# Re-ordering the opening of a four-layer modulated convolution kernel

## The chip, the cores and the metric
One core of one Trainium2 chip. The metric is the device time of one execution in microseconds, here the median of three runs.

## The reference
```python
def _layer(x, style, w, b, mw, mb, typ):
    s = style @ mw.T + mb
    weight = SCALE * w * s[:, None, :, None]
    demod = lax.rsqrt(jnp.sum(weight * weight, axis=(2, 3)) + EPS)
    weight = weight * demod[:, :, None, None]
    if typ == 'same': out = jax.vmap(_conv_same)(x, weight) + b[None, :, None]
    elif typ == 'upsample': ...  # transposed conv, stride 2, + b, then blur (1, 3, 3, 1)
    elif typ == 'downsample': ...  # blur, then conv of stride 2, + b
    return out
# layers: same, upsample, same, downsample; result is x + layer3(layer2(layer1(layer0(x))))
```
x is 128 samples of 64 channels by 1024 positions in float32, the style 128 samples by 128; each layer has 64 x 64 x 3 weights. The weights differ from sample to sample, since s and demod do.

## The kernel before
All four layers are linear, so the kernel multiplies them into one filter bank per sample, adds the identity, and applies that bank to the sample once; the few positions at the edges are computed layer by layer for 32 samples at a time (`edge`). Float32 is kept by splitting operands into a high float32r part (`high`, `w_high`, `x_high`, casts on ScalarE) and a low remainder (`low`, `w_low`, `x_low`, subtractions on VectorE), with three matmuls for a product (lines 167 to 169) or two where the low part sits in the other half of the partitions (172, 173).

Engine names: PE is TensorE, DVE VectorE, ACT ScalarE, POOL GpSimd, SP the engine that issues most of the DMAs.

Samples go in groups of four. The bank of group g comes out of seven units, `unit(g, 0)` to `unit(g, 6)`: units 0 and 1 turn Q3 (layer 3 scaled by D32) and A2 (layer 2) into Q2, units 2 and 3 with B1 (layer 1 with the blurs summed in, `static_sums`) into G, units 4 to 6 with C (layer 0) into Wf. After each unit VectorE scales the result in PSUM (`full`), ScalarE casts it, VectorE takes the low part, and only then can the unit that reads it start. `w_sum`, `w_high`, `w_low` make the taps W, and SP copies parts of W to the other half of the partitions with nine DMAs per group (`cross`, lines 217 to 227), for which the group's first sample waits. Each sample has 9 matmuls into `ps` (`conv_shared`), a copy into `py`, 15 more (`conv_rest`, one sample behind), and a result on ScalarE. POOL prepares x (`columns`, lines 608 and 609) and the Q3 of later groups (`q3_full`, `q3_low`).

The order is written out by hand, and each engine's queue is in program order: `PROLOGUE` is the list of units ahead of sample 0, `FIRST` those ahead of samples 0 to 3, `SLOTS` those of every later group; four PSUM banks are handed on along this list.

Ahead of the units stands the opening: S = style times mw (line 375), its square, the energies (line 381, three matmuls a layer), the roots and the demodulation factors DD. A factor was made of Sqrt on ScalarE (508, 513, 514), a reciprocal on VectorE (797, 826, 836) and four chained VectorE operations (`newton`, 764 to 767); each link waits for the one in front of it. D32, D10c, D21, inv3 are products of S and DD that `full`, Q3 and the identity need. Layer constants (K1, K2, K3, cv) come from small matmuls (404, 412) and short chains on VectorE (856 to 865) ahead of sample 0.

## Time and profile before
| | |
|---|---|
| median of 3 runs | 686.85 us (686.07 to 687.09) |
| the profiled execution | 686.25 us, span 684.4 us |
| busy over the span | PE 93%, DVE 81%, ACT 62%, POOL 33% |
| mean granted PE clock | 0.982 |
| chain that ended last | PE 71%, DVE 17%, ACT 6%, issue 5%, DMA 1% |
| first matmul of sample 0 / of unit (2, 4) | 55.23 / 76.27 us |

The busy shares are means over stages of different kind: an opening of some 70 us, and 31 groups after it that repeat. A share says nothing of a stage; the tables by stage and the timeline do. Times in the timeline count from the start of the span. The rest of an execution's time, 1.85 us here, lies outside the span.

### The profile page before, as it was taken

What the parts mean: (1) busy time and instruction counts of PE and PEld (TensorE: products, weight loads), DVE (VectorE), ACT (ScalarE), POOL (GpSimd) and SP (SyncE); (2) the same over time, 40 slices, a digit from 0 to 9 for tenths busy, and PEclk for the clock granted to TensorE, in tenths of its full rate; (3) what the DMA queues carried; (4) which work ended last, traced back from release to release, by engine and by line L of the source; (5) the groups of instructions that cost most, each with busy time, mean ns of one, the idle gap of its engine ahead of it and who ended that gap; (6) DMA issues with size and microseconds to landing.
All of it is one profiled execution on the core that took longest, in us unless ns stands there. A gap on an engine that the chain in (4) does not pass through costs nothing.

```text
span 684.4 us, 13324 instructions
## 1 busy us (share of the span) xinstructions
PE 635.5 (93%) x5012; PEld 626.6 (92%) x5012; DVE 551.1 (81%) x836; ACT 425.0 (62%) x713; POOL 225.6 (33%) x246
## 2 busy tenths in 40 slices
PE   5648999999999999989999999989999999989967
PEld 4647999999999999989999999989999999989967
DVE  6897687887978797978979798797988888787961
ACT  3435566576667677476666767556677757655653
POOL 4315232333234333332333333413423333224130
PEclk9987999999999999999999999999999999999999
DMA  6035388667777877757788777757886777768772
GB/s 212 38 89 136 115 231 217 178 192 194 197 197 217 231 205 200 198 167 200 189 231 227 185 194 222 199 169 197 231 215 165 221 207 213 203 166 231 196 206 108
DMA packets 155840, 129.89 MB, mean 190 GB/s; under 512 B 7104, under 2 KB 122176, under 8 KB 155776
## 3 DMA queue, kind: packets, MB, share of 16 engines
q1 hardware_dynamic: 155120, 127.47, 68.6%
q10 hardware_dynamic: 656, 1.57, 0.7%
q8 instruction: 40, 0.66, 0.4%
q14 instruction: 24, 0.20, 0.1%
HBM read 36.47 MB, written 33.82 MB: 103 GB/s over the span
## 4 chain that ended last, share of the span: by engine, by line
PE 71%; DVE 17%; ACT 6%; issue 5%; DMA 1%; POOL 0%; ACTq 0%; DVEq 0%; POOLq 0%
PE py L167 9%; PE py L169 9%; PE py L168 9%; PE ps L167 6%; PE ps L168 6%; PE pg L167 6%; PE ps L169 6%; PE pg L169 6%; PE pg L168 6%; PE pg L172 3%; PE pg L173 3%; DVE W L708 2%; DVE xl L653 1%; ACT xh L437 1%; DVE pg L661 1%
## 5 line engine op out<-in xcount | busy, mean ns | idle before, releaser
L168 PE MATMUL py<-xl,W 128*128 128x256 f32 x640 | 182.5, 285 | 0.0
L167 PE MATMUL py<-xh,W 128*128 128x256 f32 x640 | 182.4, 285 | 0.0
L169 PE MATMUL py<-xh,W 128*128 128x256 f32 x640 | 181.9, 284 | 0.0
L608 POOL TENSOR_TENSOR X<-X 128x514 f32<-128x514 f32 x64 | 73.1, 1142 | 240.3 <-DMA X<-in_xin 238.0
L167 PEld LDWEIGHTS py<-xh,W 128*128 128x128 f32 x640 | 126.9, 198 | 0.0
L168 PEld LDWEIGHTS py<-xl,W 128*128 128x128 f32 x640 | 126.8, 198 | 0.0
L169 PEld LDWEIGHTS py<-xh,W 128*128 128x128 f32 x640 | 126.7, 198 | 0.0
L486 ACT CAST W<-Wf 128x768 fp32r<-128x768 f32 x64 | 53.2, 831 | 111.6 <-PE py L169 103.7
L167 PE MATMUL ps<-xh,W 128*128 128x256 f32 x384 | 114.1, 297 | 8.7 <-issue 5.8
L653 DVE TENSOR_TENSOR xl<-X,xh 128x1548 fp32r<-128x1548 f32 x64 | 114.4, 1787 | 7.4 <-ACT xh L437 6.7
L451 ACT ACTIVATE T<-py,cv,DD 128x512 f32<-128x512 f32 x128 | 99.3, 776 | 22.4 <-PE py L169 22.4
L168 PE MATMUL ps<-xl,W 128*128 128x256 f32 x384 | 110.6, 288 | 0.0
L169 PE MATMUL ps<-xh,W 128*128 128x256 f32 x384 | 110.4, 287 | 0.0
L437 ACT CAST xh<-X 128x1548 fp32r<-128x1548 f32 x64 | 94.8, 1480 | 0.0
L167 PEld LDWEIGHTS ps<-xh,W 128*128 128x128 f32 x384 | 77.0, 200 | 10.8 <-issue 8.8
L708 DVE TENSOR_TENSOR W<-Wf,W 128x768 fp32r<-128x768 f32 x64 | 62.6, 986 | 23.5 <-ACT W L486 23.4
L592 POOL TENSOR_TENSOR Q3l<-Q3f,Q3h 128x256 fp32r<-128x256 f32 x31 | 24.1, 778 | 174.1 <-ACT Q3h L466 174.1
L443 ACT COPY py<-ps 128x512 f32<-128x512 f32 x128 | 76.0, 594 | 5.6 <-PE ps L169 5.6
L169 PEld LDWEIGHTS ps<-xh,W 128*128 128x128 f32 x384 | 77.3, 201 | 0.0
L609 POOL TENSOR_TENSOR X<-X 128x516 f32<-128x516 f32 x64 | 77.2, 1206 | 0.0
L168 PEld LDWEIGHTS ps<-xl,W 128*128 128x128 f32 x384 | 77.0, 201 | 0.0
L475 ACT CAST Q2h<-pg 128x512 fp32r<-128x512 f32 x64 | 27.5, 483 | 65.4 <-DVE pg L661 63.4
(166 smaller groups left out, 1490.5 us busy)
## 6 DMA issues: line engine op xcount, KB each, us to landing
X<-in_xin SPq DMA_DIRECT2D x64, 516.0 KB, 5.2
out<-T SPq DMA_DIRECT2D x64, 512.0 KB, 3.1
W<-W SPq DMA_DIRECT2D x64, 384.0 KB, 4.3
W<-W SPq DMA_DIRECT2D x96, 128.0 KB, 4.4
W<-M SPq DMA_DIRECT2D x96, 128.0 KB, 3.6
W<-W SPq DMA_DIRECT2D x32, 256.0 KB, 4.7
E<-in_ed ACTq DMA_DIRECT2D x1, 768.0 KB, 7.6
XE<-in_xe SPq DMA_DIRECT2D x1, 576.0 KB, 5.0
```

What stands on the lines that cost most here:

```text
L167: eng.matmul(o, wh_, rh, start=first, stop=False, skip_group_check=onto)
L168: eng.matmul(o, wh_, rl, start=False, stop=False, skip_group_check=onto)
L169: return eng.matmul(o, wl_, rh, start=False, stop=last, skip_group_check=onto)
L437: act.copy(xh[:, n % XH], X[:, n % XR, :, 1:4]).then_inc(s_xh, 1)
L443: act.copy(py[b % YR][:, :].rearrange("p (e k) -> p e k", e=2), pm.unsqueeze(1).to_broadcast([128, 2, H])).then_inc(s_ae, 1)
L451: act.activation(T[:, n % TR, q].rearrange("p e k -> p (e k)"), py[b % YR][:, :], ACT.Identity, bias=cv[:, b:b + 1], scale=DD[:, 3, b:b + ...
L475: act.copy(Q2h[:, :, 2 * u:2 * u + k], src).then_inc(s_q2h, 1)
L486: act.copy(taps_of(g, 0, k), Wf[:, :, PARTS[k]]).then_inc(s_wh, 1)
L608: pool.tensor_tensor(x[:, :, 3, 0:XW - 1], x[:, :, 0, 1:XW], x[:, :, 1, 0:XW - 1], ALU.subtract)
L609: pool.tensor_tensor(x[:, :, 2], x[:, :, 0], x[:, :, 1], ALU.subtract).then_inc(s_s, 1)
L653: tt(xl[:, n % XH], X[:, n % XR, :, 1:4], r32(xh[:, n % XH]), ALU.subtract).then_inc(s_xl, 1)
L708: m = tt(taps_of(g, 1, k), Wf[:, :, PARTS[k]], r32(taps_of(g, 0, k)), ALU.subtract)
```

## The change
1. Loads: the tables of S come as `m23` (layers 2 and 3, with the style and the biases in one transfer) and `m01`; `wt` is split (`wt2` alone on ScalarE's queue); `a2`, `wt`, `cw`, `ed` move to SP's queue, `cw`, `eye`, `ed` behind `load(0)`, and `load(2)` behind `xe`.
2. Roots: ScalarE's Abs_reciprocal_sqrt straight from PSUM, then one Newton step of three scalar_tensor_tensor operations; no reciprocal, no Sqrt. S and the energies are done in two parts, energies of layers 0, 1 and 3 in `py`.
3. Order: the prologue has group 0 whole, then (1, 0) and (1, 1). (1, 2) to (1, 6) and all that follow go into `FIRST`, a sample later than before. Constants K2 and K3 on PE stand behind samples 0 and 1 and their chains on VectorE in those samples (`constants`), the edge scales in sample 2 (`edge_scales`). `columns(0)` and `columns(1)` on POOL stand behind B1l and `identity(0)`.

The diff, cut to its core and with the indentation reduced:
```diff
-PROLOGUE = [(0, 0), (0, 1), (0, 2), (0, 3), (1, 0), (1, 1), (0, 4), (0, 5), (0, 6), (1, 2), (1, 3)]
-FIRST = [[(1, 4), (1, 5), (1, 6)], [(2, 0), (2, 1)], [(2, 2)], [(2, 3), (3, 0), (3, 1)]]
+PROLOGUE = [(0, 0), (0, 1), (0, 2), (0, 3), (0, 4), (0, 5), (0, 6), (1, 0), (1, 1)]
+FIRST = [[(1, 2), (1, 3)], [(1, 4), (1, 5), (1, 6)], [(2, 0), (2, 1)], [(2, 2), (2, 3), (3, 0), (3, 1)]]
...
+s_pp, s_ch, s_eps, s_ms, s_sq, s_ss, s_rr, s_sc, s_k0, s_b1, s_bs = (
+    sem(n) for n in ("pp", "ch", "eps", "ms", "sq", "ss", "rr", "sc", "k0", "b1", "bs"))
+PP_S23, PP_S01, PP_E2, PP_E01, PP_E3, PP_K1, PP_K2, PP_K3 = range(1, 9)
+SC_S23, SC_SQ2, SC_S01, SC_D32, SC_K1, SC_D, SC_K2, SC_K3, SC_CV = range(1, 10)
 K_A2, K_C, K_B1, K_B1D = 1, 2, 3, 4
+AT = {2: 0, 0: 1, 1: 2, 3: 3}
...
-for n, dst, src in (("mwt", MW, mwt.rearrange("p (l m) -> p l m", l=4)),
+for n, dst, src in (("m23", MS[:], m23),
                     ("b1", b1w[:, 2 * C:6 * C], b1),
-                    ("bb", BB[:], bb.rearrange("p (k l) -> p k l", k=2)),
+                    ("m01", M01, m01),
                     ("q3", q3s[:], q3.rearrange("p (k o) -> p k o", k=2)),
-                    ("eye", EYE[:], eye)):
+                    ("a2", A2f, a2),
+                    ("wt", WT[:, 1:4], wt.rearrange("p (l t m) -> p l t m", l=3, t=3))):
...
     if n == XR - 1:
-        sp.wait_ge(s_pp, 3)
+        sp.wait_ge(s_pp, PP_E3)
...
-for n in range(XR):
-    load(n)
+load(0)
+for n, dst, src in (("cw", Cf, cw.rearrange("p (d m) -> p d m", d=4)),
+                    ("eye", EYE[:], eye),
+                    ("ed", E[:], ed.rearrange("p (l t m) -> p l t m", l=4, t=3))):
+    sp.dma_start(dst, src).then_inc(s_in[n], 16)
+load(1)
 sp.dma_start(XE[:], xe).then_inc(s_in["xe"], 16)
+load(2)
 for k in range(3):
...
-for n in ("mwt", "st"):
-    pe.wait_ge(s_in[n], 16)
-for l in range(4):
-    m = pe.matmul(ps[:, l * 128:l * 128 + 128], MW[:, l, :], ST, start=True, stop=True)
+pe.wait_ge(s_in["m23"], 16)
+for l in (2, 3):
+    m = pe.matmul(pg[3][:, (l - 2) * 128:(l - 1) * 128], MS[:, (l - 2) * 128:(l - 1) * 128], ST, start=True, stop=True)
 m.then_inc(s_pp, 1)
-def energy(l):
-    o = pe_[:, 0:128] if l == 2 else ps[:, l * 128:l * 128 + 128]
+pe.wait_ge(s_in["m01"], 16)
+for l in (0, 1):
+    m = pe.matmul(ps[:, l * 128:l * 128 + 128], M01[:, l * 128:l * 128 + 128], ST, start=True, stop=True)
+m.then_inc(s_pp, 1)
+def energy(o, l):
     for t in range(3):
-        m = pe.matmul(o, SQ[:, l, t], tmp[0:64, l, :], start=t == 0, stop=t == 2)
+        m = pe.matmul(o, SQ[:, AT[l], t], tmp[0:64, l, :], start=t == 0, stop=t == 2)
     return m
...
 pe.wait_ge(s_sc, SC_SQ2)
-energy(2).then_inc(s_pp, 1)
+energy(pe_[:, 0:128], 2).then_inc(s_pp, 1)
 pe.wait_ge(s_sq, 2)
-pe.wait_ge(s_ss, 1)
-for l in (0, 1, 3):
-    m = energy(l)
-m.then_inc(s_pp, 1)
+pe.wait_ge(s_ss, 2)
+energy(py[0][:, 0:128], 0)
+energy(py[0][:, 128:256], 1).then_inc(s_pp, 1)
+energy(py[1][:, 0:128], 3).then_inc(s_pp, 1)
 pe.wait_ge(s_a2, 1)
-for i in range(YR):
-    pe.matmul(py[i][:, :], A2h[:, 0:128], A2h[:, :], start=True, stop=True)
 for x in PROLOGUE[:2]:
...
 pe.wait_ge(s_b1, 1)
-for x in PROLOGUE[2:6]:
+for x in PROLOGUE[2:4]:
     unit(*x)
+pe.wait_ge(s_cl, 1)
+for x in PROLOGUE[4:]:
+    unit(*x)
+pe.wait_ge(s_sc, SC_D)
+for i in range(YR):
+    pe.matmul(py[i][:, :], A2h[:, 0:128], A2h[:, :], start=True, stop=True)
 pe.wait_ge(s_in["ed"], 16)
-pe.wait_ge(s_sc, SC_K1)
 for t in range(3):
...
 m.then_inc(s_pp, 1)
-pe.wait_ge(s_cl, 1)
-for x in PROLOGUE[6:]:
-    unit(*x)
-for l, k, at in ((2, 1, SC_K2), (3, 3, SC_K3)):
+def constant(l, k, at):
     pe.wait_ge(s_sc, at)
     for t in range(3):
-        m = pe.matmul(pe_[0:64, 0:128], WT[:, l, t], tmp[0:64, k, :], start=t == 0, stop=t == 2)
+        m = pe.matmul(pe_[0:64, 0:128], WT[:, AT[l], t], tmp[0:64, k, :], start=t == 0, stop=t == 2)
     m.then_inc(s_pp, 1)
...
+    if b == 0:
+        constant(2, 1, SC_K2)
+    elif b == 1:
+        constant(3, 3, SC_K3)
     if i == 3 and g % 2 == 0:
...
 def _(act):
-for n, dst, src in (("st", ST, st), ("wt", WT, wt.rearrange("p (l t m) -> p l t m", l=4, t=3)),
...
-act.wait_ge(s_one, 1)
-act.activation(one[:], one[:], ACT.Sqrt)
-act.wait_ge(s_in["wt"], 16)
-twice = lambda l: WT[:, l].unsqueeze(2).to_broadcast([64, 3, 2, C])
...
-act.activation(pairs(2), twice(2), ACT.Square).then_inc(s_sq, 1)
+def square(a, e):
+    return act.activation(SQ[:, a:e].rearrange("p l t (d m) -> p (l t) d m", d=2),
+                          WT[:, a:e].rearrange("p l t m -> p (l t) m").unsqueeze(2).to_broadcast(
+                              [64, 3 * (e - a), 2, C]), ACT.Square).then_inc(s_sq, 1)
+def root(r, e):
+    return act.activation(r, e, ACT.Abs_reciprocal_sqrt, bias=eps[:, 0:1]).then_inc(s_rr, 1)
+act.wait_ge(s_eps, 1)
+act.activation(RR[:, 0, 0:1], eps[:], ACT.Abs_reciprocal_sqrt)
+act.wait_ge(s_in["wt2"], 16)
+square(0, 1)
 act.wait_ge(s_in["a2"], 16)
...
-for l in (0, 1):
-    act.activation(pairs(l), twice(l), ACT.Square)
-act.activation(pairs(3), twice(3), ACT.Square).then_inc(s_sq, 1)
-act.wait_ge(s_sc, SC_S)
-act.activation(tmp[:, 0:2], S[:, 0:2], ACT.Square)
+act.wait_ge(s_in["wt"], 16)
+square(1, 4)
+act.wait_ge(s_sc, SC_S23)
 act.activation(tmp[:, 3], S[:, 3], ACT.Square).then_inc(s_ss, 1)
-act.wait_ge(s_sc, SC_A2)
-act.activation(RR[:, 2, :], AA[:, 2, :], ACT.Sqrt).then_inc(s_ss, 1)
+act.wait_ge(s_sc, SC_S01)
+act.activation(tmp[:, 0:2], S[:, 0:2], ACT.Square).then_inc(s_ss, 1)
+act.wait_ge(s_pp, PP_E2)
+root(RR[:, 2], pe_[:, 0:128])
 act.wait_ge(s_in["cw"], 16)
 act.copy(Ch[:], Cf).then_inc(s_k0, 1)
+act.wait_ge(s_pp, PP_E01)
+root(RR[:, 0:2], py[0][:, 0:256].rearrange("p (l b) -> p l b", l=2))
+act.wait_ge(s_pp, PP_E3)
+root(RR[:, 3], py[1][:, 0:128])
 q3_high(0)
-act.wait_ge(s_sc, SC_A)
-act.activation(RR[:, 0:2, :], AA[:, 0:2, :], ACT.Sqrt)
-act.activation(RR[:, 3, :], AA[:, 3, :], ACT.Sqrt).then_inc(s_ss, 1)
 act.wait_ge(s_bs, 6)
...
 q3_high(1)
-x_high(0)
 high(0, 2)
 high(0, 3)
+x_high(0)
+w_high(0, 0)
+w_high(0, 1)
+w_high(0, 2)
 high(1, 0)
 high(1, 1)
-for k in range(3):
-    w_high(0, k)
-high(1, 2)
-high(1, 3)
-x_high(1)
 q3_high(2)
...
     if b >= 2:
+        if b == 2:
+            act.wait_ge(s_sc, SC_CV)
         result(b - 2)
-    else:
-        act.wait_ge(s_sc, SC_CV)
-    if b == 0:
+    if b == 1:
         q3_full(3)
     n = b // Q + 1
-    if b % Q == 0 and 2 <= n < NQ:
+    if b % Q == 0 and n < NQ:
         x_high(n)
...
-columns(0)
-columns(1)
 pool.wait_ge(s_k0, K_B1)
...
 m.then_inc(s_b1, 1)
+columns(0)
+pool.wait_ge(s_sc, SC_D32)
 q3_full(1)
+pool.tensor_tensor(Cl[:], Cf, r32(Ch[:]), ALU.subtract).then_inc(s_cl, 1)
 q3_low(1)
-pool.tensor_tensor(Cl[:], Cf, r32(Ch[:]), ALU.subtract).then_inc(s_cl, 1)
 pool.wait_ge(s_sc, SC_D)
...
 identity(0)
+columns(1)
+pool.wait_ge(s_c, cnt(1, 1))
 q3_full(2)
...
         m.then_inc(s_ed, 1)
-def newton(l):
-    link(tt(tmp[:, l], RR[:, l], RR[:, l], ALU.mult))
-    link(tt(tmp[:, l], tmp[:, l], AA[:, l], ALU.mult))
-    link(dve.tensor_scalar(tmp[:, l], tmp[:, l], -0.5, 1.5, ALU.mult, ALU.add))
-    link(tt(DD[:, l], tmp[:, l], RR[:, l], ALU.mult))
-psv = ps[:, :].rearrange("p (l b) -> p l b", l=4)
+def newton(l, e):
+    link(dve.scalar_tensor_tensor(out=tmp[:, l], in0=e, scalar=EPS, in1=RR[:, l], op0=ALU.add, op1=ALU.mult))
+    link(dve.scalar_tensor_tensor(out=tmp[:, l], in0=tmp[:, l], scalar=-0.5, in1=RR[:, l], op0=ALU.mult, op1=ALU.mult))
+    link(dve.scalar_tensor_tensor(out=DD[:, l], in0=tmp[:, l], scalar=1.5, in1=RR[:, l], op0=ALU.add, op1=ALU.mult))
+two = lambda ap: ap[:, 0:256].rearrange("p (l b) -> p l b", l=2)
 bsum = [b1w, b1p, 0]
...
 dve.wait_ge(s_ms, 1)
-static_sums(3)
-dve.wait_ge(s_in["bb"], 16)
-dve.wait_ge(s_pp, 1)
-reached(tt(S[:], psv, bc(BB[:, 1, :], B), ALU.add))
-dve.wait_ge(s_sc, SC_S)
+static_sums(1)
+dve.wait_ge(s_pp, PP_S23)
+reached(tt(S[:, 2:4], two(pg[3]), bc(BB[:, 1, 2:4], B), ALU.add))
+dve.wait_ge(s_sc, SC_S23)
 reached(tt(tmp[:, 2], S[:, 2], S[:, 2], ALU.mult))
+static_sums(1)
+dve.wait_ge(s_pp, PP_S01)
+reached(tt(S[:, 0:2], two(ps), bc(BB[:, 1, 0:2], B), ALU.add))
+static_sums(1)
 tt(D21[:], S[:, 1], S[:, 2], ALU.mult)
-static_sums(1)
-dve.wait_ge(s_pp, 2)
-reached(dve.tensor_scalar(AA[:, 2], pe_[:, 0:128], EPS, None, ALU.add))
-dve.wait_ge(s_k0, K_A2)
-tt(A2l[:], A2f, r32(A2h[:]), ALU.subtract).then_inc(s_a2, 1)
-dve.wait_ge(s_ss, 2)
-link(dve.reciprocal(RR[:, 2], RR[:, 2]))
-newton(slice(2, 3))
+dve.wait_ge(s_rr, 1)
+newton(2, pe_[:, 0:128])
 reached(tt(D32[:], DD[:, 2], S[:, 3], ALU.mult))
...
 m.then_inc(s_q3f, 1)
-dve.wait_ge(s_pp, 3)
-dve.tensor_scalar(AA[:, 0:2], psv[:, 0:2], EPS, None, ALU.add)
-reached(dve.tensor_scalar(AA[:, 3], psv[:, 3], EPS, None, ALU.add))
+dve.wait_ge(s_k0, K_A2)
+tt(A2l[:], A2f, r32(A2h[:]), ALU.subtract).then_inc(s_a2, 1)
 dve.wait_ge(s_q3h, 1)
...
 lone_low(dve, Q3h[hi, :, 1], Q3f[hi, :, 1]).then_inc(s_q3l, 1)
-static_sums(2)
+static_sums(3)
 full(0, 0)
 full(0, 1)
+dve.wait_ge(s_rr, 2)
+dve.tensor_scalar(AA[:, 0], py[0][:, 0:128], EPS, None, ALU.add)
+newton(slice(0, 2), two(py[0]))
 low(0, 0)
 low(0, 1)
+dve.tensor_scalar(tmp[:, 0], DD[:, 1], bias(0), None, ALU.mult)
+reached(dve.scalar_tensor_tensor(out=D10c[:], in0=DD[:, 0], scalar=1.0 / 32.0, in1=DD[:, 1],
+                                 op0=ALU.mult, op1=ALU.mult))
 dve.wait_ge(s_k0, K_B1D)
...
 m.then_inc(s_b1d, 1)
-dve.wait_ge(s_ss, 3)
-link(dve.reciprocal(RR[:, 0:2], RR[:, 0:2]))
-newton(slice(0, 2))
-dve.tensor_scalar(tmp[:, 0], DD[:, 1], bias(0), None, ALU.mult)
-reached(dve.scalar_tensor_tensor(out=D10c[:], in0=DD[:, 0], scalar=1.0 / 32.0, in1=DD[:, 1],
-                                 op0=ALU.mult, op1=ALU.mult))
+dve.wait_ge(s_rr, 3)
+dve.tensor_scalar(AA[:, 3], py[1][:, 0:128], EPS, None, ALU.add)
+newton(3, py[1][:, 0:128])
 dve.wait_ge(s_sc, SC_K1)
 full(0, 2)
+reached(tt(inv3[:], AA[:, 3], DD[:, 3], ALU.mult))
+low(0, 2)
 full(0, 3)
-low(0, 2)
 low(0, 3)
-link(dve.reciprocal(RR[:, 3], RR[:, 3]))
-newton(slice(3, 4))
-reached(tt(inv3[:], AA[:, 3], DD[:, 3], ALU.mult))
-full(1, 0)
-full(1, 1)
-dve.tensor_scalar(tmp[:, 1], S[:, 2], bias(1), 2.0, ALU.mult, ALU.mult)
-dve.wait_ge(s_pp, 4)
-link(tt(kt[lo], pe_[0:64, 0:128], D21[lo], ALU.mult))
-reached(tt(tmp[lo, 1], tmp[lo, 1], kt[lo], ALU.add))
-low(1, 0)
-low(1, 1)
 full(0, 4)
...
     w_low(0, k)
+full(1, 0)
+full(1, 1)
 x_low(0)
-dve.wait_ge(s_pp, 5)
-link(tt(kt[lo], pe_[0:64, 0:128], DD[lo, 2, :], ALU.mult))
-link(dve.tensor_scalar(kt[lo], kt[lo], BB[lo, 0, 2:3], None, ALU.add))
-reached(tt(tmp[lo, 3], kt[lo], S[lo, 3, :], ALU.mult))
-link(tt(b0z[:], AA[:, 0], DD[:, 0], ALU.mult))
-tt(D10[:], DD[:, 0], DD[:, 1], ALU.mult)
-dve.tensor_scalar(b0z[:], b0z[:], bias(0), None, ALU.mult)
-dve.wait_ge(s_pp, 6)
-link(tt(cv[lo], pe_[0:64, 0:128], DD[lo, 3, :], ALU.mult))
-link(dve.tensor_scalar(cv[lo], cv[lo], BB[lo, 0, 3:4], None, ALU.add))
-reached(dve.tensor_copy(cv[hi], cv[lo]))
-full(1, 2)
-full(1, 3)
-low(1, 2)
-low(1, 3)
-x_low(1)
-dve.wait_ge(s_in["xe"], 16)
-dve.wait_ge(s_ms, 2)
-edge_in(0)
+low(1, 0)
+low(1, 1)
+dve.tensor_scalar(tmp[:, 1], S[:, 2], bias(1), 2.0, ALU.mult, ALU.mult)
+dve.wait_ge(s_pp, PP_K1)
+link(tt(kt[lo], pe_[0:64, 0:128], D21[lo], ALU.mult))
+reached(tt(tmp[lo, 1], tmp[lo, 1], kt[lo], ALU.add))
+def constants(k):
+    if k == 0:
+        dve.wait_ge(s_pp, PP_K2)
+        link(tt(kt[lo], pe_[0:64, 0:128], DD[lo, 2, :], ALU.mult))
+        link(dve.tensor_scalar(kt[lo], kt[lo], BB[lo, 0, 2:3], None, ALU.add))
+        reached(tt(tmp[lo, 3], kt[lo], S[lo, 3, :], ALU.mult))
+    else:
+        dve.wait_ge(s_pp, PP_K3)
+        link(tt(cv[lo], pe_[0:64, 0:128], DD[lo, 3, :], ALU.mult))
+        link(dve.tensor_scalar(cv[lo], cv[lo], BB[lo, 0, 3:4], None, ALU.add))
+        reached(dve.tensor_copy(cv[hi], cv[lo]))
+def edge_scales():
+    link(tt(b0z[:], AA[:, 0], DD[:, 0], ALU.mult))
+    tt(D10[:], DD[:, 0], DD[:, 1], ALU.mult)
+    dve.tensor_scalar(b0z[:], b0z[:], bias(0), None, ALU.mult)
+    dve.wait_ge(s_in["xe"], 16)
+    dve.wait_ge(s_ms, 2)
+    edge_in(0)
 for b in range(B):
...
     us = units_of(b)
-    if i == 1 and g + 1 < NGR:
+    behind = b and (g + 1, 4) in units_of(b - 1)
+    if behind:
         w_low(g + 1, 1)
...
     n = (b + 1) // Q
-    if b % Q == 1 and 2 <= n < NQ:
+    if b % Q == 1 and n < NQ:
         x_low(n)
+    if b in (0, 1):
+        constants(b)
+    elif b == 2:
+        edge_scales()
     for x in us:
...
             low(*x)
-    if i == 0 and g + 1 < NGR:
+    if (g + 1, 4) in us:
         w_low(g + 1, 0)
-    elif i == 1 and g + 1 < NGR:
+    if behind:
         w_low(g + 1, 2)
```

## Rows read from the trace of the kernel before

**Rows 1.** Table by stages: us, busy time (instructions) by engine, clock, DMA share, GB/s.
```profile
core 0: us, PE busy (x) PEld busy (x) DVE busy (x) ACT busy (x) POOL busy (x), PEclk, DMA share, GB/s
...
50.00:55.00 5.00, 4.55 (x21) 4.58 (x22) 4.43 (x6) 2.10 (x4) 2.69 (x3) 0.50 0.88 224
60.00:70.00 10.00, 6.75 (x44) 6.58 (x43) 4.88 (x9) 5.09 (x8) 4.33 (x5) 0.83 0.78 181
70.00:90.00 20.00, 20.00 (x165) 19.99 (x165) 15.22 (x22) 13.09 (x23) 5.92 (x5) 1.00 0.45 135
```

**Rows 2.** DMA issues to landing, then timeline: start us, us, engine, line, operation.
```profile
T<-in_cw ACTq DMA_DIRECT2D x1, 256.0 KB, 5.6
...
T<-in_wt ACTq DMA_DIRECT2D x1, 192.0 KB, 4.5
...
7.77 0.93 ACT L502 ACTIVATE X<-T 64x384 f32<-64x384 f32 x2
...
9.76 4.18 PE L381 MATMUL ps<-tmp,X 64*128 64x128 f32 x18 [0.46 <-ACT tmp L506]
```

**Rows 3.** Timeline of the opening, VectorE and GpSimd side by side.
```profile
11.20 0.29 DVE L764 TENSOR_TENSOR tmp<-RR 128x128 f32<-128x128 f32 x1
...
11.52 1.08 DVE L765 TENSOR_TENSOR tmp<-tmp,AA 128x128 f32<-128x128 f32 x1
12.41 1.15 POOL L609 TENSOR_TENSOR X<-X 128x516 f32<-128x516 f32 x1
12.63 1.01 DVE L766 TENSOR_SCALAR tmp<-tmp 128x128 f32<-128x128 f32 x1
```

**Rows 4.** Timeline, checkpoints A and B and what stands between.
```profile
17.80 0.42 DVE L176 TENSOR_TENSOR Q3h<-Q3f,Q3h 64x256 fp32r<-64x256 f32 x1
...
20.53 1.03 DVE L661 TENSOR_TENSOR pg<-pg,D 128x512 f32<-128x512 f32 x2 [0.66 <-PE pg L173]
20.91 1.96 POOL L615 TENSOR_TENSOR B1l<-b1s,B1h 128x384 fp32r<-128x384 f32 x2 [5.19 <-ACT B1h L517]
...
23.18 0.55 PE L167 MATMUL pg<-Q2h,B1h 128*128 128x256 f32 x1 [2.33 <-DVE Q2h L176]
```

**Rows 5.** Timeline, low parts and reciprocal behind checkpoint B.
```profile
23.44 0.92 DVE L821 TENSOR_TENSOR B1dl<-b1s,B1dh 64x128 fp32r<-64x128 f32 x2 [0.41 <-ACT B1dh L525]
...
25.87 1.75 DVE L826 RECIPROCAL RR<-RR 128x256 f32<-128x256 f32 x1
...
26.50 1.27 POOL L619 TENSOR_TENSOR Cl<-T,Ch 128x512 fp32r<-128x512 f32 x1
```

**Rows 6.** VectorE's groups by form, 9 to 66 us: busy us, mean ns.
```profile
L708 DVE TENSOR_TENSOR W<-Wf,W 128x768 fp32r<-128x768 f32 x4 | 3.6, 942 | 0.0
L653 DVE TENSOR_TENSOR xl<-X,xh 128x1548 fp32r<-128x1548 f32 x2 | 3.5, 1764 | 0.5 <-ACT xh L437 0.5
...
L715 DVE TENSOR_TENSOR b1s<-XE,S 128x288 f32<-128x288 f32 x1 | 1.0, 991 | 0.0
```

**Rows 7.** Timeline, checkpoints C and D, first copy of W, first sample.
```profile
32.29 0.43 DVE L176 TENSOR_TENSOR Gh<-pg,Gh 64x256 fp32r<-64x256 f32 x1
...
41.88 1.81 DVE L708 TENSOR_TENSOR W<-Wf,W 128x768 fp32r<-128x768 f32 x2
...
42.91 0.70 SPq L217 DMA_DIRECT2D W<-W  x1
...
55.23 0.28 PE L167 MATMUL ps<-xh,W 128*128 128x256 f32 x1
```

**Rows 8.** The last of W's nine copies (line 227).
```profile
L227 SPq DMA_DIRECT2D W<-M x1: 624/624/624, 50.7 to 50.7; - x1
...
DMA to landing us min/median/max: 3.1/3.1/3.1
```

**Rows 9.** Timeline of PE, unit (2, 2) and unit (2, 4).
```profile
63.92 0.36 PE L167 MATMUL pg<-Q2h,B1h 128*128 128x256 f32 x1 [3.25 <-DVE Q2h L176]
...
76.27 0.44 PE L167 MATMUL pg<-Gh,Ch 128*128 128x256 f32 x1
```

34 lines of the change are left out of this document (15 added, 19 removed).

## The prediction
> **What bounds the kernel now.** I read the table by stages first. From 70 us on PE is busy in all of its time (20.00 of 20 us, 165 matmuls, clock 1.00); before that it is not: 6.75 of 10 us at 60 to 70, and it runs at a lower granted clock there (0.83, and 0.50 at 50 to 55, which is 1.2 GHz of 2.4) [rows 1]. The reader is to see that the steady part is TensorE's and that the opening isn't: at 50 to 55 DVE is busy 4.43 of 5 us, and PE, at half its pace, waits for it at either end. Everything the diff edits lies in the opening, so its worth is the shift of one point, the first matmul of unit (2, 4), at 76.27 us [rows 9]: up to it both kernels issue the same units and samples, behind it the same stream. The profiled execution took 686.25 us (span 684.4), the median is 686.85; I shift the profile's point and carry the shift to the median.
>
> I then followed the timeline of the opening over all engines, with four checkpoints: **A**, Q3h complete for unit (0, 0), at 18.22; **B**, first matmul of (0, 2), 23.18 [rows 4]; **C**, Gh's low part complete, 32.72; **D**, first `w_low` of group 0 done, 42.8, whereupon SP starts the nine copies of W and sample 0 starts at 55.23 [rows 7].
>
> **What goes.** Three reciprocals (1.75 for 256 elements [rows 5], about 0.95 for each of the two of 128) and one of four Newton operations, some 1.0: 4.7 us of DVE. And `columns(0)`, `columns(1)` leave 11.4 to 15.7 us, where four chained DVE operations took 1.01 to 1.08 instead of 0.29 [rows 3]: 3.1 us. Together 7.8. The question is what is given back.
>
> **Step A.** `wt` is now the sixth issue on SP, near 3.1 us. Before it landed 4.5 us after its issue, at 1.19 [rows 2]; with fewer bytes in front I take 7.0 (6.5 to 7.6). Three layers squared at once 1.2 (two separately 0.93 [rows 2]), S squared 0.7: energies from 8.9, against 9.76. They keep PE for 4.18 us [rows 2]: 13.1. `q3_high(0)` now stands behind the root of layer 3 on ScalarE, and so behind that 13.1: root 0.3, cast 0.6, DVE's two low parts 0.85: A at 15.0, a gain of 3.2. D32 is ready at 10.3 instead of 15.9, but waits for this queue. The function behind the root is not in the trace; at 0.3 us I cost it as the Sqrt it replaces. Sqrt, Square and Copy now run on one table load of 1.28 us; if the new function's table lacked Square or Copy, two or three reloads would come on top, ahead of A. I take none, since nothing but the anchor function changes, and keep 1.3 to 3.8 for the upper end.
>
> **Hidden edits.** `S` in two pieces costs DVE 0.15 more (0.42 twice for 0.69), beside PE's first matmuls. `a2`, `cw` and `ed` go from ScalarE's queue to SP's, `cw` and `ed` behind `load(0)`: issued near 4.2 and landing in the 5.6 us of before or less [rows 2], `cw` is there at 8.7 to 9.8, where ScalarE wants it at 9.2 for Ch; `ed` lands near 11 and PE wants it after 36. `load(2)` now stands behind `xe`, and waits for the energies as before; `columns(2)` wants it after 43. The table load moves from 3.3 to 1.2 us and nobody waits for it. If `cw` were late by 2 us still, ScalarE's next work (the root of layers 0 and 1, at 11.7) would not be touched, so all this is costed at nothing. Three scalar_tensor_tensor operations replace four; at 128 elements one took 0.28, as much as a tensor_tensor, so I price them alike (bounds 0.28 and, for 256 elements, 0.45).
>
> **Step B.** Three static sums (2.3) run to 17.3 while PE does (0, 0). Then DVE: `full` twice 1.03 [rows 4], AA[0] 0.3, Newton for layers 0 and 1 on 256 elements 3 x 0.45, `low` twice 1.15: 21.2 if nothing interferes. POOL has B1l (1.96 [rows 4]) from 18.4, and two of the Newton operations read SBUF twice: plus 0.8. B at 22.1, gain 1.1; AA and Newton now stand ahead of `low`.
>
> **The lock, which decides.** Rows 3 show the rule of the trace: L765 and L766, alone 0.29, end 0.1 us after the GpSimd operation that was running (13.64 against 13.56). L661 beside L615, with its first input in PSUM, isn't stretched: 1.03 for 512 and 256 elements [rows 4]. B1dl's first pair took 0.92 instead of 0.56 beside POOL [rows 5]. In the new order POOL works without a pause from 18.4 to about 27.5: B1l 1.96, `columns(0)` 2.2 (two like L609 [rows 3]), Q3f 1.2, Cl 1.27 [rows 5], Q3 low parts 1.6. In that time DVE issues ten operations with both inputs in SBUF. Going through them in turn, one DVE operation for each of POOL's, two where POOL itself waits for a semaphore, the scale, D10c and B1dl's six end at 27.2 instead of 24.5: 2.7 us. All lock terms ahead of D: 0.8 + 2.7 + 0.4 (a W sum and `w_low` beside `q3_full(2)`) = 3.9; bounds 0, and 4.8 with strict alternation.
> [...]
>
> **Steps C and D.** (0, 2) may end only with B1dl: 27.8; (0, 3) ten matmuls at the slow pace of 0.217 (21 in 4.55 us [rows 1]), since PE idles ahead of it: 29.9. DVE goes on from B1dl with AA 0.3, Newton 0.95, `full(0, 2)` 0.7: 29.15. Then copy 0.6, `low` 0.7, `full(0, 3)` 0.7, copy 0.6, two lows 0.85, one after the other where before paired them: C at 32.6, gain 0.1. From there before needed 10.1 us to D, since (1, 0), (1, 1), Newton 3 and K2 lay between. Now: `full(0, 4)` 0.7, sum 0.45, wait for (0, 5) 0.8, `full` 0.7, identity 0.45, two sums 0.9, `full(0, 6)` 0.5, `w_low` 0.93 (prices [rows 4, 6]), lock 0.4: **D at 38.4, gain 4.4**.
>
> **From D to sample 0.** The nine copies start with L217 at 42.91 and the last lands at 50.7 + 3.1 = 53.8 [rows 7, 8]: 10.95 after D. Before, PE filled this with (1, 4) to (1, 6) and started 1.4 later. Now W is there at 49.35, and DVE's two `w_low`, `full(1, 0)`, `(1, 1)`, `x_low(0)` and lows (5.2 [rows 6]) let (1, 2) start at 43.7, so that its and (1, 3)'s 24 matmuls, two thirds at the slow pace, end at 48.5: sample 0 at 49.4, 5.9 earlier.
>
> **What is given back.** The cover is gone: `constants(0)` on DVE waits for PE's matmuls, which stand behind sample 0. Behind that wait are `low(1, 2)` and `low(1, 3)`, for which PE's (1, 4) waits. The chain: sample 0 1.25, constant 0.85, DVE 0.9, `low` 0.7, (1, 4) 1.4, then `full` and sums of (1, 4..6) 3.9, `x_low(1)` 1.7 [rows 6], `constants(1)` 0.85, two `w_low` 1.8, `full(2, 0)`, `(2, 1)` 1.0, `edge_scales` 0.8 + 0.99 (L715 [rows 6]), lows 1.15: 17.3 from 49.35, so `low(2, 1)` ends at 66.6 at best. Before it released PE at 63.92. POOL meanwhile has `q3_low(3)` and `columns(3)` from 61.9 to 67 (it was held until then by `q3_high(3)`, which stands on ScalarE behind PE's (2, 1)), across `edge_scales`: by the same count plus 2.2 (bounds 0 and 2.8): 68.8. PE has ended sample 1's rest at 64 and idles nearly 5 us (before 3.25 [rows 9]).
> What is left to (2, 4): before 82 matmuls and the edge in 12.35, of which 82 x 0.12 + 1.0 are work and 1.5 the lower clock (granted 0.83 over 60 to 70 [rows 1]). Now 58 matmuls: 6.95 + 1.0 + 1.5 = 9.5. **(2, 4) at 78.3, against 76.27: plus 2.0.** I take 1.9: 688.7.
> In short: D 4.4 earlier, then 39.9 us to (2, 4) where before took 33.5. D must come before 36.4 for the change to pay.
>
> **Rivals.**
> 1. The collisions mostly miss: phases shift by a few tenths and POOL's operations fall beside DVE's PSUM ones. For it: before, only some nine DVE operations of the opening were stretched. Against: POOL has no pause here. All of 3.9 + 2.2 = 6.1 us gone gives 682.7, half of it 685.8. This is the case on the other side: below 4.1 us of lock the kernel is faster than before, below 2.7 measurably. Band 682.7 to 685.5.
> 2. Partly so: 2.7 to 5.5 us of lock. The work removed is paid back and the end stays: 685.5 to 688.2.
> 3. PE's clock falls also in the idle 1.6 us ahead of (1, 4). Before it stood low after 3.2 us without work and did not fall after 1.2. Then the chain is 1.5 longer, with `wt` late 0.6: 690.8.
>
> **How the numbers follow.** 0.2% (1.4 us) is what a measurement of this kernel can tell from no change. Forecast (lock as the rows have it) 0.37, its own range 688.2 to 690.2; rival 1 0.27; rival 2 0.28; rival 3 0.08. So faster 0.27, same 0.28, slower 0.45. The forecast is the likeliest single case, by little. Both signs hold much of the chance, so the range leaves out only the deep end of rival 1 and the top of rival 3: 683.5 to 690.9.
>
> **What would show it.** Right: D near 38.4; B1dl's and `edge_scales`'s operations 0.5 to 1.1 us beside POOL; Q3h's cast released by the root behind the energies; sample 0's first matmul near 49.4; PE waiting some 5 us for Q2h ahead of (2, 2); (2, 4) at 78. Wrong: (2, 4) before 76; B1dl at 0.28 each; or a stall in the steady part that before hasn't.

## The result and the profile after

The changed kernel takes 691.7 us (median of 6 runs, 689.0 to 692.46), the kernel before 687.0 beside it; the ratio is 1.0058, 95% interval 1.0038 to 1.0078: 0.6% slower. The forecast was 688.7 with a range up to 690.9, so the side was right and the size was not: 691.7 lies above the range. The profiled execution took 692.25 us, span 690.4. Executions of one kernel scatter by 2 to 3 us either way (the kernel before from 684.31 to 689.78 in 26), so a single profile is read for the place of its points, and the ratios for the time.

The checkpoints of the prediction, in us, of the two profiles and of the forecast:

| | before | forecast | after |
|---|---|---|---|
| A, Q3h complete for (0, 0) | 18.22 | 15.0 | 15.66 |
| B, first matmul of (0, 2) | 23.18 | 22.1 | 22.91 |
| C, Gh's low part complete | 32.72 | 32.6 | 33.65 |
| D, first `w_low` of group 0 done | 42.8 | 38.4 | 39.1 |
| sample 0, first matmul | 55.23 | 49.4 | 50.04 |
| `low(2, 1)` complete | 63.8 | 68.8 | 70.30 |
| (2, 4), first matmul | 76.27 | 78.3 | 80.72 |

(D is read as half of the pair that `w_low` is shown in: it starts at 38.21 and takes some 0.9.) The work taken away is seen: sample 0 starts 5.2 us earlier. So is what is given back: from sample 0 to (2, 4) the kernel before takes 21.0 us, the changed one 30.7. From (2, 4) to the end of the span it is 608.1 and 609.7, which is within the scatter.

The timeline of the changed kernel, VectorE and GpSimd, in the stretch of [rows 3 to 5] (start us, us, engine, line, operation, elements):
```profile
15.24 0.42 DVE L179 TENSOR_TENSOR Q3h<-Q3f,Q3h 64x256 fp32r<-64x256 f32 x1
...
19.14 2.15 POOL L633 TENSOR_TENSOR B1l<-b1s,B1h 128x384 fp32r<-128x384 f32 x2 [14.55 <-ACT B1h L539]
...
19.20 0.41 DVE L787 SCALAR_TENSOR_TENSOR tmp<-py,RR 128x256 f32<-128x256 f32 x1
19.65 0.77 DVE L788 SCALAR_TENSOR_TENSOR tmp<-tmp,RR 128x256 f32<-128x256 f32 x1
20.46 1.12 DVE L789 SCALAR_TENSOR_TENSOR DD<-tmp,RR 128x256 f32<-128x256 f32 x1
...
21.23 1.29 POOL L628 TENSOR_TENSOR X<-X 128x514 f32<-128x514 f32 x1
22.49 1.09 POOL L629 TENSOR_TENSOR X<-X 128x516 f32<-128x516 f32 x1
22.79 0.88 DVE L837 TENSOR_SCALAR tmp<-DD,MS 128x128 f32<-128x128 f32 x1
...
23.59 0.72 DVE L838 SCALAR_TENSOR_TENSOR D10c<-DD 128x128 f32<-128x128 f32 x1
24.23 1.97 DVE L845 TENSOR_TENSOR B1dl<-b1s,B1dh 64x128 fp32r<-64x128 f32 x2
...
26.14 0.80 DVE L846 TENSOR_TENSOR B1dl<-b1s,B1dh 64x128 fp32r<-64x128 f32 x1
26.95 0.99 DVE L845 TENSOR_TENSOR B1dl<-b1s,B1dh 64x128 fp32r<-64x128 f32 x2
```
L787 reads its first input from PSUM and isn't stretched beside POOL (0.41 for 256 elements); L788 and L789 read SBUF twice and take 0.77 and 1.12. Then the operations of 128 elements, 0.28 alone, take 0.7 to 1.0 each; L837 ends at 23.67, 0.1 us behind L629's 23.58. Being stretched beside GpSimd, which the prediction calls the lock, adds 1.0 in Newton and, against 0.28 each, 3.4 from L837 to the last L845. GpSimd is at its queue all this time, until 27.6; the last of the B1dl operations, behind that, took 0.28.

The same view, from sample 0 to unit (2, 4), PE with it, for [rows 6, 7, 9]:
```profile
50.04 0.37 PE L170 MATMUL ps<-xh,W 128*128 128x256 f32 x1 [0.93 <-issue]
...
52.21 0.28 DVE L878 TENSOR_TENSOR kt<-pe,DD 64x128 f32<-64x128 f32 x1 [2.37 <-PE pe L425]
...
53.05 0.68 DVE L712 TENSOR_TENSOR Gl<-pg,Gh 128x512 fp32r<-128x512 f32 x1
...
53.87 0.36 PE L170 MATMUL pg<-Gh,Ch 128*128 128x256 f32 x1 [1.70 <-DVE Gl L712]
...
65.52 0.71 DVE L888 TENSOR_TENSOR b0z<-AA,DD 128x128 f32<-128x128 f32 x1
66.15 1.09 POOL L628 TENSOR_TENSOR X<-X 128x514 f32<-128x514 f32 x1
66.26 1.14 DVE L889 TENSOR_TENSOR D<-DD 128x128 f32<-128x128 f32 x1
67.21 1.15 POOL L629 TENSOR_TENSOR X<-X 128x516 f32<-128x516 f32 x1
67.32 1.12 DVE L890 TENSOR_SCALAR b0z<-b0z,MS 128x128 f32<-128x128 f32 x1
68.36 0.88 DVE L737 TENSOR_TENSOR b1s<-XE,S 128x288 f32<-128x288 f32 x1
...
69.87 0.43 DVE L179 TENSOR_TENSOR Q2h<-pg,Q2h 64x256 fp32r<-64x256 f32 x1
...
70.44 0.55 PE L170 MATMUL pg<-Q2h,B1h 128*128 128x256 f32 x1 [4.25 <-DVE Q2h L179]
...
80.72 0.44 PE L170 MATMUL pg<-Gh,Ch 128*128 128x256 f32 x1
```
`constants(0)` (L878) waits 2.37 us for PE's constant, which stands behind sample 0, and behind it `low(1, 2)` keeps PE from (1, 4). The edge scales (L888 to L737, 65.52 to 69.24) take 3.7 us between `full(2, 1)` and `low(2, 1)`, and for that last low part PE stands 4.25 us.

The table by stages of the changed kernel, for [rows 1] (columns as there: PE, its weight load, DVE, ACT, POOL, then PE's granted clock, DMA share, GB/s):
```profile
50.00:55.00 5.00, 3.26 (x24) 2.94 (x25) 2.20 (x6) 2.23 (x6) 0.00 (x0) 1.00 0.19 71
55.00:60.00 5.00, 5.00 (x32) 5.00 (x30) 3.46 (x8) 1.48 (x3) 0.00 (x0) 0.66 0.00 0
...
65.00:70.00 5.00, 1.20 (x10) 0.99 (x9) 4.93 (x8) 3.01 (x5) 3.77 (x5) 0.88 0.90 205
70.00:75.00 5.00, 4.55 (x21) 4.59 (x22) 1.43 (x3) 0.46 (x1) 0.00 (x0) 0.50 0.94 179
```
The clock falls twice. At 55 to 60 it is 0.66: 16 matmuls at 0.21 us each instead of 0.12, behind the idle 1.7 us ahead of (1, 4). At 70 to 75, behind the idle 4.25 us, it is 0.50, the level of 1.2 GHz: 21 matmuls in 4.55 us, PE "busy" all the time.

### The profile page after: what moved, and what is told of

Same layout as the page of the kernel before. It is cut to its first block, busy times and chain, and to the rows that moved or that the text cites. A ratio compares the mean times of both kernels' runs of the same rounds, so it can differ in the third digit from the quotient of the medians.

```text
span 690.4 us, 13316 instructions
## 1 busy us (share of the span) xinstructions
PE 638.3 (92%) x5012; PEld 628.9 (91%) x5012; DVE 544.5 (79%) x830; ACT 425.0 (62%) x711; POOL 223.3 (32%) x246
## 4 chain that ended last, share of the span: by engine, by line
PE 71%; DVE 17%; ACT 5%; issue 5%; DMA 1%; SPq 0%; ACTq 0%; DVEq 0%
PE py L170 9%; PE py L172 9%; PE py L171 9%; PE ps L170 6%; PE pg L170 6%; PE pg L172 6%; PE pg L171 6%; PE ps L171 5%; PE ps L172 5%; PE pg L175 3%; PE pg L176 3%; DVE W L730 2%; DVE pg L683 1%; DVE xl L675 1%; ACT xh L452 1%
## 5 line engine op out<-in xcount | busy, mean ns | idle before, releaser
L628 POOL TENSOR_TENSOR X<-X 128x514 f32<-128x514 f32 x64 | 73.5, 1149 | 239.2 <-DMA X<-in_xin 236.9
L171 PEld LDWEIGHTS py<-xl,W 128*128 128x128 f32 x640 | 128.2, 200 | 0.0
L675 DVE TENSOR_TENSOR xl<-X,xh 128x1548 fp32r<-128x1548 f32 x64 | 113.8, 1778 | 6.9 <-ACT xh L452 6.2
L170 PEld LDWEIGHTS ps<-xh,W 128*128 128x128 f32 x384 | 76.0, 198 | 12.0 <-issue 10.1
L172 PEld LDWEIGHTS ps<-xh,W 128*128 128x128 f32 x384 | 76.3, 199 | 0.0
L629 POOL TENSOR_TENSOR X<-X 128x516 f32<-128x516 f32 x64 | 74.7, 1167 | 0.0
L170 PE MATMUL pg<-Q2h,B1h 128*128 128x256 f32 x192 | 57.0, 297 | 15.0 <-DVE Q2h L179 15.0
```

The source lines that it names most:

```text
L170: eng.matmul(o, wh_, rh, start=first, stop=False, skip_group_check=onto)
L171: eng.matmul(o, wh_, rl, start=False, stop=False, skip_group_check=onto)
L172: return eng.matmul(o, wl_, rh, start=False, stop=last, skip_group_check=onto)
L628: pool.tensor_tensor(x[:, :, 3, 0:XW - 1], x[:, :, 0, 1:XW], x[:, :, 1, 0:XW - 1], ALU.subtract)
L629: pool.tensor_tensor(x[:, :, 2], x[:, :, 0], x[:, :, 1], ALU.subtract).then_inc(s_s, 1)
L675: tt(xl[:, n % XH], X[:, n % XR, :, 1:4], r32(xh[:, n % XH]), ALU.subtract).then_inc(s_xl, 1)
```

## The experiments

The theory: the order of the change gives back more than the removed work brings, in three places: the edge scales ahead of `low(2, 1)` (their work, the lock, and TensorE's lower clock behind the wait), the constants ahead of `low(1, 2)`, and GpSimd's columns beside VectorE's small operations. The rivals: that the loads and roots bring nothing or harm; that the clock alone makes the loss; that one place alone does. Nothing of the computation is left out in any kernel; e7 adds matmuls whose result nobody reads. The ratio is to the kernel before, run on the same chip; e1 to e4, e5 to e8 and e9 to e12 ran on a chip each. The points are of the one profiled execution, `low(2, 1)` its end, (2, 4) and sample 0 their first matmul.

| kernel | sample 0 | `low(2, 1)` | (2, 4) | ratio, 95% interval |
|---|---|---|---|---|
| the change | 50.04 | 70.30 | 80.72 | 1.0058, 1.0038 to 1.0078 |
| e1 constants late | 51.59 | 68.86 | 79.74 | 1.0052, 1.0031 to 1.0073 |
| e2 edge scales late | 50.38 | 66.63 | 74.77 | 1.0001, 0.9984 to 1.0018 |
| e3 columns early | 49.03 | 68.00 | 77.63 | 1.0064, 1.0040 to 1.0089 |
| e4 GpSimd held | 49.45 | 67.16 | 75.31 | 1.0012, 0.9995 to 1.0028 |
| e5 all three | 49.77 | 64.23 | 72.36 | 0.9934, 0.9908 to 0.9959 |
| e6 loads and roots only | 53.12 | 61.31 | 72.33 | 0.9938, 0.9917 to 0.9958 |
| e7 clock held | 50.10 | 69.11 | 77.24 | 1.0016, 0.9993 to 1.0039 |
| e8 e6, edge scales late | 51.56 | 60.09 | 72.60 | 0.9955, 0.9934 to 0.9976 |
| e9 e1 and e2 | 50.80 | 65.24 | 73.37 | 0.9955, 0.9939 to 0.9972 |
| e10 e2 and e3 | 48.92 | 65.13 | 73.25 | 0.9982, 0.9963 to 1.0001 |
| e11 reciprocals back | 50.80 | 71.09 | 81.41 | 1.0096, 1.0067 to 1.0124 |
| e12 e6, columns late | 55.04 | 63.23 | 74.25 | 0.9997, 0.9981 to 1.0014 |

The points are rougher than they look, since the clock falls at other places in other executions. Ahead of sample 0 the change, e1 to e5, e7 and e9 to e11 run the same instructions on PE, yet in (0, 4) to (0, 6) the matmuls start 0.21 apart in e1, e2 and e9 (in e11 some of them) and 0.12 apart in the others. So from C to the start of the first `w_low` it is 5.8, 5.4 and 5.4 us in the first three and 4.6 in the change.

**The edge scales.** In e2 they stand behind the low parts and `w_low` of sample 2's turn on VectorE, instead of ahead of them:
```diff
-                elif b == 2:
-                    edge_scales()
...
                 if behind:
                     w_low(g + 1, 2)
+                if b == 2:
+                    edge_scales()
```


> The changed kernel with one edit: the edge scales of sample 2 stand behind low(2, 0), low(2, 1) and w_low(1, 2) instead of ahead. Theory 'order': low(2, 1) ends 3.6 us earlier (66.7 for 70.3), PE's wait for it shrinks from 4.3 to about 0.7, and the slow spell behind it (24 matmuls at 0.214 instead of 0.12, 2.3 us) goes too: unit (2, 4) at 75 to 77, time 4 to 6 us below the changed kernel, at or below the kernel before. Rival, 'the clock falls anyway': 3.6 us only. Theory 'lock' alone: the four operations have lost 1.8 us to GpSimd, the rest of their time doesn't count: 1.8 us.

Measured 1.0001, 0.57% under the change. The timeline of e2's PE, first matmul of (2, 2):
```profile
66.78 0.36 PE L170 MATMUL pg<-Q2h,B1h 128*128 128x256 f32 x1 [1.69 <-DVE Q2h L179]
```
PE idles 1.69 us instead of 4.25 (0.7 was expected), and the matmuls behind go at 0.12: the clock of e2 is 1.00 from 60 to 80 us. `low(2, 1)` comes 3.7 earlier, (2, 4) 6.0, more than the 3.9 us of the ratio; this execution is also without the slow matmuls behind (1, 4). By its ratio this is the largest single piece of the loss.

e4 leaves the edge scales where they are and takes only the collision away, by holding GpSimd:
```diff
+                if b == 1:
+                    pool.wait_ge(s_ed, 1)
                 if b % Q == 0 and XR - 1 <= n < NQ:
                     columns(n)
```

> The changed kernel with GpSimd held ahead of q3_low(3) and columns(3) until the edge scales are done, so that only the collision is taken away and the order stays. Theory 'lock': the edge scales (65.5 to 69.2, 3.6 us) shrink to 1.8, low(2, 1) ends 1.8 earlier, and the time is 1.8 to 2.3 below the changed kernel. If collisions there cost nothing, or GpSimd's delay comes back later (unit (3, 0) waits for its Q3l), no change or slower.

Its timeline of VectorE:
```profile
64.93 0.28 DVE L890 TENSOR_TENSOR b0z<-AA,DD 128x128 f32<-128x128 f32 x1
65.25 0.29 DVE L891 TENSOR_TENSOR D<-DD 128x128 f32<-128x128 f32 x1
65.45 0.28 DVE L892 TENSOR_SCALAR b0z<-b0z,MS 128x128 f32<-128x128 f32 x1
65.65 0.45 DVE L739 TENSOR_TENSOR b1s<-XE,S 128x288 f32<-128x288 f32 x1
```
The same four operations take 1.2 us (64.93 to 66.10) instead of 3.7, with no change of their own. PE waits 1.70 us instead of 4.25 and the matmuls behind start 0.12 apart. The ratio falls by 0.46% to 1.0012, 3.2 us, where 1.8 to 2.3 was expected. So the collision with what follows from it (PE's wait and the clock) is worth about as much as moving the edge scales away altogether. The two intervals don't part e4 from e2, so what the work itself costs stays open.

e7 leaves both and fills PE's wait with 18 matmuls of 512 columns into a free bank:
```diff
+                if b == 3:
+                    pe.wait_ge(s_sc, SC_CV)
+                    for _ in range(18):
+                        pe.matmul(pe_[:, :], A2h[:, 0:128], A2h[:, :], start=True, stop=True)
                 for x in units_of(b):
```


> The changed kernel with 18 matmuls of 512 columns into an unused PSUM bank while PE waits for low(2, 1) ahead of unit (2, 2); their results are not read. The wait stays. Theory: of the distance from low(2, 1) to unit (2, 4), 10.3 us, 2.3 are the lower clock behind the wait; with PE kept at work the 24 matmuls from 70.4 run at 0.12 instead of 0.214: unit (2, 4) 2.0 to 2.3 us earlier, time 2 us below the changed kernel. Rival: the clock falls by its own phase, and nothing changes.

The timeline of its PE:
```profile
64.60 4.26 PE L433 MATMUL pe<-A2h 128*128 128x512 f32 x18
69.26 0.35 PE L170 MATMUL pg<-Q2h,B1h 128*128 128x256 f32 x1 [0.41 <-DVE Q2h L179]
69.45 0.28 PE L171 MATMUL pg<-Q2l,B1h 128*128 128x256 f32 x1
```
The starts lie 0.12 apart at once, where the change has 24 at 0.214. From `low(2, 1)` to (2, 4) it takes 8.1 us instead of 10.4, and the ratio is 1.0016, 0.42% under the change. The low clock behind the wait is worth 2.3 us here by the points; the forecast had 1.5. (e7's (2, 4) is 3.5 us earlier than the change's; the other 1.2 were gained ahead of `low(2, 1)`, where the clock was 1.00 from 55 to 60 us in this execution and not 0.66.)

**The constants.** e1 puts them behind the low parts of the sample's units:
```diff
-                if b in (0, 1):
-                    constants(b)
-                elif b == 2:
+                if b == 2:
                     edge_scales()
                 for x in us:
                     if x[1] < 4:
                         low(*x)
+                if b in (0, 1):
+                    constants(b)
```


> The changed kernel with one edit: on VectorE the constants of K2 stand behind low(1, 2) and low(1, 3) instead of ahead of them. Theory 'order': PE's unit (1, 4) no longer waits for sample 0 and a constant (it started at 53.9, PE was free at 52.2), so low(1, 2) is done by 50.6 and unit (2, 4) moves from 80.7 to 79.0, or to 77.5 if the slow spell of PE at 55.3 to 58.7 goes with the idle time. Time 1.7 to 3.2 us below the changed kernel. Theory 'lock' (only the collisions of VectorE and GpSimd cost): no change beyond 0.3 us.

Measured 1.0052, where 1.7 to 3.2 us less were expected: nothing that its interval can tell from the change, though `low(2, 1)` came 1.4 us earlier and (2, 4) 1.0. PE no longer waits ahead of (1, 4), and from sample 0 to `low(2, 1)` it is 17.3 us instead of 20.3, but PE waits 4.49 us ahead of (2, 2), no less than the change's 4.25, with 23 slow matmuls behind. (Sample 0 itself is 1.5 us later in this execution, by the slow (0, 4) to (0, 6).) With the edge scales late too (e9), the constants do count:

> Two of e5_three's three edits: constants behind the lows and edge scales behind w_low, the columns as in the change. e5 stood 0.67% below e2 (edge late alone). If that comes from the constants behind the lows, which lets PE's (1, 4) start earlier once nothing else delays it: ratio to before 0.993 to 0.996, low(2, 1) ends at 64 to 65.5. Rival, that it comes from the early columns: ratio 0.998 to 1.001, low(2, 1) near 66.6 as in e2.

0.9955, 0.46% under e2; `low(2, 1)` at 65.24. Its timeline of VectorE shows the order turned round, the low parts first:
```profile
51.00 0.68 DVE L712 TENSOR_TENSOR Gl<-pg,Gh 128x512 fp32r<-128x512 f32 x1
...
52.95 0.28 DVE L878 TENSOR_TENSOR kt<-pe,DD 64x128 f32<-64x128 f32 x1 [0.32 <-PE pe L425]
```
`low(1, 2)` runs at 51.0, against 53.44 in e2, and VectorE waits 0.32 us for PE's constant, against 1.87. By the points this is 1.4 us of (2, 4); the ratio says 3.2 us, with 1.6 either way.

**The columns.** e3 puts `columns(0)` and `columns(1)` back ahead of B1l on GpSimd:
```diff
+            columns(0)
+            columns(1)
             pool.wait_ge(s_k0, K_B1)
             for h in range(2):
...
             m.then_inc(s_b1, 1)
-            columns(0)
...
             identity(0)
-            columns(1)
```


> The changed kernel with columns(0) and columns(1) back ahead of B1l on GpSimd. Theory 'lock': GpSimd is free 2.3 us earlier behind B1l, the scale, D10c and B1dl (22.8 to 28.1) get 1.5 to 2.5 us back, the collisions that appear at 10 to 13 us instead are hidden by VectorE's wait for Q3h (2.3 us): first w_low ends 1.5 to 2 us earlier than 39.2 and so does unit (2, 4). Time 1.5 to 2 us below the changed kernel. Rival: Q3f, Cl and Q3l alone cover the same operations, so less than 0.7 us comes back.

Measured 1.0064, no gain, though (2, 4) came 3.1 us earlier in its profiled execution: the one kernel whose point and ratio, both taken against the kernel before, disagree by more than 2 us. Some 2 us of the 3.1 are the clock: no slow matmuls behind (1, 4), and 15 instead of 24 behind (2, 2), after a wait of 4.48 us. The first `w_low` starts 1.0 earlier, 1.5 to 2 were expected. A comes 0.7 later and C 1.0 earlier: the collision is moved from the B1dl operations onto the Q3 ones, and a little less is left of it.

> The other two of e5_three's edits: edge scales behind w_low and the columns of GpSimd at their place of before, the constants as in the change. If the early columns are what e5 had over e2: ratio 0.993 to 0.996. If the constants are: ratio 0.998 to 1.001, low(2, 1) at 66 to 67.

0.9982, 0.19% under e2, which the two intervals can't tell from nothing. This is what was expected if the constants are what e5 (below) has over e2, though `low(2, 1)`, at 65.13, came 0.9 us ahead of the range given for it; e9 says the same from the other side.

> The changed kernel with three edits at once: K2's chain and the edge scales behind the low parts, and columns(0), columns(1) back at the start of GpSimd. Theory 'order': late edge scales alone brought the time from 1.006 of before to 1.000; the early columns take 1 us off the first w_low in the trace, K2's place another 1 to 1.5 off unit (1, 4). Unit (2, 4) at 72.5 to 74, time 0.996 to 0.999 of before. Rival: PE's next wait takes their place (W of group 1 or the lows behind full(2, 1)), and the time stays at 1.000.

e5 is the sum: 0.9934, lower than was expected. The three undone places give 1.24% against the change: 0.57 for the edge scales and, each on top of them, 0.46 for the constants (e9) and 0.19 for the columns (e10), which add up to 1.22. Without the edge scales moved, the constants (e1) and the columns (e3) gave nothing measurable; PE's wait ahead of (2, 2) was 4.5 us in both, with slow matmuls behind it. Why the time of e1 and e3 kept nothing of their earlier (2, 4) isn't shown. e5's table by stages:
```profile
50.00:60.00 10.00, 10.00 (x81) 9.39 (x81) 7.97 (x17) 4.43 (x10) 0.00 (x0) 1.00 0.05 19
60.00:70.00 10.00, 8.32 (x70) 8.15 (x69) 8.87 (x16) 6.47 (x12) 5.04 (x5) 1.00 0.77 180
70.00:80.00 10.00, 10.00 (x81) 9.99 (x81) 8.25 (x14) 5.50 (x11) 2.34 (x2) 1.00 0.53 164
```
PE does 232 matmuls in these 30 us, at full clock throughout; the changed kernel does 164 in them.

**The roots and loads alone.** e6 has the loads and roots of the change and the order of before on every engine (the `PROLOGUE` and `FIRST` of before, the columns ahead of B1l, the constants and edge scales ahead of sample 0; S and the energies stay in two parts):
```diff
-PROLOGUE = [(0, 0), (0, 1), (0, 2), (0, 3), (0, 4), (0, 5), (0, 6), (1, 0), (1, 1)]
-FIRST = [[(1, 2), (1, 3)], [(1, 4), (1, 5), (1, 6)], [(2, 0), (2, 1)], [(2, 2), (2, 3), (3, 0), (3, 1)]]
+PROLOGUE = [(0, 0), (0, 1), (0, 2), (0, 3), (1, 0), (1, 1), (0, 4), (0, 5), (0, 6), (1, 2), (1, 3)]
+FIRST = [[(1, 4), (1, 5), (1, 6)], [(2, 0), (2, 1)], [(2, 2)], [(2, 3), (3, 0), (3, 1)]]
```


> Loads and roots of the change (parts 1 and 2 of it, the energies and S in two pieces) with the order of units, columns, constants and edge scales of the kernel before. If the removed work lay on the path and the order alone gave it back: reciprocals and one Newton operation for 256 and 128 elements are 3.4 us of VectorE between 18 and 35, the first Q3h comes 2.5 us earlier, so sample 0 at 50 to 51 (55.2 before), unit (2, 4) at 71 to 73 (76.3 before), time 3.5 to 5 us below before. Rival: the removed work was hidden, and the loads or roots cost something themselves: within 1 us of before.

0.9938: 0.6% faster than before. (2, 4) is at 72.33, 3.9 earlier than before, as expected, but sample 0 is at 53.12, not at 50 to 51. So what the loads and roots take away was on the path, and the order costs 1.2% on top of it (1.0058 over 0.9938), as much as the three places together. Its timeline of VectorE still has collisions, in other places:
```profile
10.27 1.07 DVE L812 TENSOR_TENSOR D<-DD,S 128x128 f32<-128x128 f32 x1
...
15.30 1.21 DVE L179 TENSOR_TENSOR Q3h<-Q3f,Q3h 64x256 fp32r<-64x256 f32 x1
...
21.92 1.30 DVE L833 TENSOR_TENSOR B1dl<-b1s,B1dh 64x128 fp32r<-64x128 f32 x2 [0.41 <-ACT B1dh L541]
...
25.49 1.50 DVE L782 SCALAR_TENSOR_TENSOR tmp<-tmp,RR 128x256 f32<-128x256 f32 x1
```

e11 is the reverse: the change with a reciprocal back in front of each Newton group, so that of the roots' edit only the fourth Newton operation stays out.
```diff
-                return act.activation(r, e, ACT.Abs_reciprocal_sqrt, bias=eps[:, 0:1]).then_inc(s_rr, 1)
+                return act.activation(r, e, ACT.Sqrt, bias=eps[:, 0:1]).then_inc(s_rr, 1)
...
             def newton(l, e):
+                link(dve.reciprocal(RR[:, l], RR[:, l]))
```


> The changed kernel with ScalarE's function back to Sqrt and a reciprocal on VectorE in front of each of the three Newton groups (0.95 us for 128 elements, 1.75 for 256), so with the new loads and the new order alone. If the removed VectorE work was really on the path and the order gave back more than it: the first w_low of group 0 starts about 3 us later than in the changed kernel (41 against 38.2), (2, 4) 1.5 to 3 us later (82 to 84), and the time is 1.0 to 1.9 us or more above the changed kernel's 691.7, ratio to before 1.008 to 1.011. Rival, that the reciprocals lie beside waits in this order and that the roots bring nothing here: ratio within 0.001 of the changed kernel's 1.0058.

1.0096, as expected of the ratio; the points are not: the first `w_low` starts 0.8 us later than in the change, not 3, though 3.6 us of work came back. Its timeline of VectorE shows where it went:
```profile
8.67 0.95 DVE L786 RECIPROCAL RR<-RR 128x128 f32<-128x128 f32 x1 [0.85 <-ACT RR L514]
...
18.08 1.74 DVE L786 RECIPROCAL RR<-RR 128x256 f32<-128x256 f32 x1
...
25.58 1.01 DVE L845 TENSOR_TENSOR B1dl<-b1s,B1dh 64x128 fp32r<-64x128 f32 x2
26.52 0.27 DVE L846 TENSOR_TENSOR B1dl<-b1s,B1dh 64x128 fp32r<-64x128 f32 x1
26.81 0.49 DVE L845 TENSOR_TENSOR B1dl<-b1s,B1dh 64x128 fp32r<-64x128 f32 x2
27.22 0.29 DVE L846 TENSOR_TENSOR B1dl<-b1s,B1dh 64x128 fp32r<-64x128 f32 x1
```
The first reciprocal lies ahead of the wait for the energies, beside nothing that is late. The second pushes the B1dl operations behind GpSimd's, where they take 1.9 us instead of 3.9. (A is at 14.53 here and 15.66 in the change, with the loads landing at other times; 1.1 us of the difference is that.) The point of (2, 4) moves by 0.7 us and the ratio by 0.38%, 2.6 us, and the two intervals allow from almost nothing to 5, so how much of their 3.6 us the reciprocals are worth in this order stays open.

**Two that should have been better still.** e8 is e6 with the edge scales moved from ahead of sample 0 to behind the low parts of sample 1's turn:
```diff
-            link(tt(b0z[:], AA[:, 0], DD[:, 0], ALU.mult))
-            tt(D10[:], DD[:, 0], DD[:, 1], ALU.mult)
-            dve.tensor_scalar(b0z[:], b0z[:], bias(0), None, ALU.mult)
...
-            edge_in(0)
...
                 if behind:
                     w_low(g + 1, 2)
+                if b == 1:
+                    edge_scales()
```


> As the run with loads and roots alone, and the edge scales moved out of the opening to behind sample 1's low parts on VectorE. Theory: edge scales and products (1.9 us, more beside GpSimd) stood on VectorE's path to low(2, 1) also in the kernel before; PE's wait ahead of (2, 2), 3.3 us before, falls below 2. Time another 1.5 to 2 us below the run with loads and roots alone. Rival: they then delay full and w_low of group 1 or 2, and nothing is gained.

It missed: 0.9955, not below e6's 0.9938, and the intervals don't part them. PE's wait ahead of (2, 2) is 2.87 us against 2.89 in e6, where below 2 was expected. Sample 0 comes 1.6 us and `low(2, 1)` 1.2 earlier (1.2 of it already at A, which the edit doesn't touch), but (2, 4) is at 72.60 against 72.33: some 17 matmuls between sample 0 and there run at the slow pace, against one or two in e6.

e12 is e6 with GpSimd's queue in the order of the change, B1l first and the columns behind:
```diff
-            columns(0)
-            columns(1)
             pool.wait_ge(s_k0, K_B1)
...
             m.then_inc(s_b1, 1)
+            columns(0)
```


> The loads and roots of the change with the order of before on all engines except GpSimd, which has the order of the change: B1l first, columns(0) and columns(1) behind it. If the collisions of the columns with the Newton and Q3l operations at 10 to 16 us cost e6_roots_only its share (its Newton operation took 1.50 instead of 0.45), checkpoint A comes some 1 to 1.5 us earlier than e6's 16.5 and the time falls by 0.5 to 1.5 us, to 681.5 to 682.5 and a ratio of 0.991 to 0.993. Rival, that the columns now collide with the low parts of B1d instead, as they do in the changed kernel: (2, 4) within 1 us of e6's 72.3 and the ratio 0.993 to 0.995.

It missed too, and by more than its rival had: 0.9997, 0.6% above e6. A comes 1.05 us earlier and B 1.0, as expected, since the Q3 operations are free of GpSimd. Then:
```profile
20.88 2.33 DVE L835 TENSOR_TENSOR B1dl<-b1s,B1dh 64x128 fp32r<-64x128 f32 x2 [0.42 <-ACT B1dh L541]
23.14 0.69 DVE L836 TENSOR_TENSOR B1dl<-b1s,B1dh 64x128 fp32r<-64x128 f32 x1
23.84 1.89 DVE L835 TENSOR_TENSOR B1dl<-b1s,B1dh 64x128 fp32r<-64x128 f32 x2
25.65 0.81 DVE L836 TENSOR_TENSOR B1dl<-b1s,B1dh 64x128 fp32r<-64x128 f32 x1
```
B1dl takes 5.6 us instead of 2.8 in e6, PE waits 2.6 us for it, and sample 0 starts 1.9 later. One edit of GpSimd's queue, without any new work, costs 0.6% in this order.

No version beats e5 and e6 (0.9934 and 0.9938), which beat both kernels; e8 and e9 (0.9955) can't be told from them by their intervals. e5 keeps the change's order of the units and e6 has the order of before, so that part of the new order costs nothing that these runs can measure.

## Why the prediction was off in size

**What failed** is the term for the lower clock in the last stretch: "of which 82 x 0.12 + 1.0 are work and 1.5 the lower clock ... Now 58 matmuls: 6.95 + 1.0 + 1.5 = 9.5". The 1.5 was carried over from the kernel before, where PE had idled 3.25 us, came back at full pace, and 16 matmuls went slow from 65.4 on. Measured, the stretch took 10.4 us, and 24 of its matmuls ran at 0.214 instead of 0.12, from the first on: 2.3 us. e7, which takes only this away, shortened the stretch by 2.3 and the time by 0.42%. The size isn't fixed: behind waits of 4.3 to 4.5 us, e11, e1 and the change have 22 to 24 slow matmuls and e3 has 15. With the spell behind (1, 4), below, the slow clock is 3.8 us behind sample 0 in this execution, where 1.5 was costed.

**Rival 3 came on top.** It said that the clock falls also in the idle time ahead of (1, 4), for 1.5 us, and had a chance of 0.08. PE idled 1.7 there and 16 matmuls went at 0.21, 1.5 us. The runs show that this happens in some executions only: at 55 to 60 us the clock is 0.66 in the change and in e11 and 0.71 in e4, but 1.00 in e2, e3, e7 and e10, where the same matmuls stand behind the same constants. No run holds the clock there, so what this spell is worth is read from the trace alone. Its time, 690.8, is near the result, but not by its own sum alone: the larger clock term above is in the result too.

**The chain from sample 0**, "17.3", with 2.2 of lock across the edge scales, was to end 19.4 behind sample 0; it ended 20.3 behind. The edge scales took 3.7 us against 4.0 forecast, so the difference of 0.9 lies ahead of them, in (1, 4) to (1, 6) at the low clock.

**Step A** was 0.66 late and B, C, D and sample 0 with it (0.6 to 1.1). The energies started at 9.66, not 8.9: `wt` was forecast to land at 7.0 (6.5 to 7.6); issued at 3.08, it landed 4.7 us later, at 7.8, and ScalarE started its squares at 7.84. A2h's cast, which the prediction left out and which had waited for `a2` until 7.17, ended at the same moment, so it cost nothing more. In the five other kernels that have this opening unchanged `wt` lands between 7.2 and 8.1, the squares start behind it, and A goes with it: 15.05 to 15.95 over the six.

**The lock** was right in place, and 0.9 and 0.3 low in size. Up to B1dl's end it took 4.4 us, against 3.5 forecast for that part, and across the edge scales 2.5 (3.7 against e4's 1.2), forecast 2.2. Of the ten operations that the prediction counts as having both inputs in SBUF, the scale (L837) is a TENSOR_SCALAR with one tensor, as L766 is in [rows 3]; both were stretched all the same. The Trainium skill ("SBUF — State Buffer", "Who interferes with whom") says that a VectorE instruction with two SBUF inputs contends with a GpSimd instruction that reads SBUF, and that the shared port pair is an exclusive lock. e4 bears this out: 3.7 us with GpSimd at work, 1.2 with GpSimd held, the instructions being the same. Rivals 1 and 2, that it mostly or partly misses, are out; for them it was to be below 5.5 us, and it was 6.9. e4, which leaves 4.4 of it, stands at 1.0012, about where the prediction's point of 4.1 put the kernel before.

**What goes**: 7.8 us of VectorE work and collisions ahead of D, of which D got 3.7 (4.4 forecast). e6 shows that in the order of before the loads and roots together are worth 0.6%, so the loss is not theirs. The function behind the root reloaded no table: the change has one table load, at 1.3 us, of 1.28. Its roots took 0.35, 0.47 and 0.37 against 0.3.

**The stall** ahead of (2, 2) was 4.25 us, forecast "nearly 5".

**Hidden edits**: `cw` let ScalarE wait 0.43 us for Ch, at 9.8, with nobody behind it; `ed`, `eye` and `load(2)` weren't waited for. No stall came into the steady part.

**The range** left out the top of rival 3, at 690.9. Added up, the terms that were low are 0.6 up to sample 0, 0.9 between it and `low(2, 1)` and 0.9 in the last stretch, 2.4 in all, and 78.3 became 80.7. The last two, mostly the clock's, are 1.8 of the 2.4.

## What to carry to other kernels

An order of work that takes a wait off one engine's queue mostly puts it on another's: cost it by what stands behind the moved instructions, as here `low(2, 1)` behind the edge scales, and try the moved pieces by themselves and in pairs, since three small ones together ate twice what the shorter work brought, and the constants showed only once the edge scales were out of the way. Where PE idles, cost the matmuls that follow at the slow pace too, as a range: from a stretch with as long a wait, and from more than one execution. And small VectorE operations on SBUF beside a GpSimd queue without pauses cost as much as GpSimd's operations do, nearly one for one here; moving GpSimd's work is then an edit worth as much as removing VectorE's.

## What the runs showed of the hardware

- A TENSOR_SCALAR with one tensor as its input is stretched beside GpSimd as the two-input operations are: L890 took 1.12 in the change and 0.28 with GpSimd held (L892 in e4), L837 0.88. The Trainium skill ("SBUF — State Buffer", "Who interferes with whom") has this too: it lists `tensor_scalar` among those that can enter a mode that takes the shared ports.
- In a collision the engine that was first went on and the other waited. A GpSimd queue without pauses loses little to short VectorE operations: its columns took 1.09 to 1.29 beside the B1dl chain and 1.09 to 1.11 alone at 31 and 45 us, B1l 2.15 against 1.95 to 1.96 in e12 and before. But where one started just behind a long VectorE operation with both inputs in SBUF, it was the one that waited: L628 of the change took 2.66 us instead of 1.10 and ended 1.0 behind L675.
```profile
77.77 1.76 DVE L675 TENSOR_TENSOR xl<-X,xh 128x1548 fp32r<-128x1548 f32 x1
77.82 2.66 POOL L628 TENSOR_TENSOR X<-X 128x514 f32<-128x514 f32 x1 [8.90 <-DMA X<-in_xin]
```
- The clock fell behind an idle 1.7 us ahead of (1, 4) in the change and, in the same place, not in e2 (idle there for 1.7 too; its matmuls from 54.3 to 59.7 start 0.12 apart), nor in e3, e7 and e10. What tells the executions apart wasn't found; one profile of each kernel can't say how often it happens.
- The row of granted clock can't be relied on in the first 30 to 37 us of these profiles: in the change it reads 1.00 from 15 to 30 us while the matmuls from 16.2 to 30.7 start 0.21 apart, and in e2 still at 33.7 to 36.7. The distance between the starts shows the pace.
- Step A moves by 0.9 us (15.05 to 15.95) between kernels whose opening is the same up to there; the loads land at different times.
